# A pipelined image tower on one core: the same pieces in another order on five queues

## The chip, the cores and the metric

The kernel runs on one core of a Trainium2 chip. The metric is the device time of one execution in microseconds. Three runs of the kernel before took 1986.72, 1967.69 and 1971.06 us, so the median is 1971.06 us.

## The reference

The input x holds 128 images of 64 x 64 positions with 128 channels, in float32. The reference computes, one stage after the other:

```
h = avgpool8x8(depthwise_conv3x3(x, conv_w) + conv_b)           # 64 tokens of 128 channels per image
h = h + attention(layernorm(h))                                  # one head, L0
h = h + shared_experts(n) + top2_of_8_experts(n),  n = layernorm(h)   # hidden width 512, exact gelu
h = h + attention(layernorm(h))                                  # 8 heads, rotary, 64 own + 15 pooled keys + sink, L1
h = h + W2 @ gelu(W1 @ layernorm(h) + b1) + b2                   # channel mixing, L1
```

The output is 128 x 64 x 128 values in float32. x is 268 MB, and it is read once.

## The kernel before, in words

**Groups and stages.** The images are taken in 16 groups of eight (512 tokens, four tiles of 128). A group passes through four stages: tok (load, pool, convolution), att (first attention and the gate of the experts), ffn (experts) and sec (second attention and channel mixing). The loop over i is a software pipeline. In iteration i, tok works on group i, att on i-1, ffn on i-2 and sec on i-3 (function `stages`). There are 19 iterations, 0 to 18, and all four stages are at work in iterations 3 to 15. Work named with a mark (out') belongs to the iteration before and is done in the next.

**The order.** Each engine runs one written list of pieces in each iteration, the dict ORDER at lines 57 to 97: `sp` for SyncE, `pe` for TensorE, `act` for ScalarE, `dve` for VectorE, `pool` for GpSimd. A piece is a few instructions with the semaphore waits that they need. Within an engine nothing overtakes, and between engines only semaphores bind. So the order decides what a wait holds up, and the data flow does not depend on it.

**The pieces of tok.** load.u.v (line 378) brings 2 MB of x into one of two buffers (v), four times in a group (u); before it SyncE waits until TensorE has read what the buffer held. pair (DVE, L1063), two add (GpSimd, L1363), inner (ACT L759, then DVE L1067) and pool (PE, L446, L449, L454) follow on each load. tap.p.n (DVE, L1084, L1091) are the 30 steps of the convolution on pooled data, out (PE L418) turns the result.

**The pieces of att.** att.0 (DVE moments, then GpSimd, L1335), att.1 (DVE L1055, then PE and ACT) and on to att.12; high, low and rest split the normalised rows in two bf16 halves; scatter.0 to 7 (GpSimd, L1352) write the rows to their experts' places in memory.

**The pieces of ffn.** up.q and down.q are the shared experts. moe (DVE L1215) takes their sum out of the bank that lift.0 then writes. For each of 15 blocks of 128 rows there are lift.j (PE L564, ACT L836), widen.j (PE L579 to L581, ACT L845 with gelu), narrow.j (PE L591, L595, ACT L855) and store.j (SyncE, L404, 64 KB). Both expert weights of a block are found by a register that TensorE reads at the head of widen (`value_load`, L571). rows.0 to 2 (L397) bring back the scattered rows. Two banks alternate: widen.j waits until narrow.j-2 has been copied out. There are five output slots: narrow.j on ScalarE waits until store.j-5 has landed (L854).

**The pieces of sec.** gather.0 to 7 (GpSimd, L1374) wait for all 15 stores, mix adds, pre.1 to pre.7 and split make keys and values, score.n, exp, turn.n and value.n are the attention in eight halves, post.0 to post.5 the rest. score.0 waits for split and for pre.7 on ScalarE; value.n+1 waits for value.n on VectorE; exp waits for score.7.

**SyncE's queue.** One list holds loads and stores. A store that is issued behind a load lies behind its 2 MB.

## Time and profile before

| | us |
|---|---|
| median of three runs | 1971.06 |
| the profiled execution | 2000.31 |
| its span, first to last instruction | 1998.4 |
| iterations 0 to 2 (filling the pipeline) | 0 to 295 |
| iterations 3 to 15 (all stages) | 295 to 1698 |
| iterations 16 to 18 (draining) | 1698 to 1998 |

The iterations are told apart by the first matmul of up.0 (L526). The profiled execution is 29 us longer than the median of the runs. TensorE is busy 85% of the span, VectorE 65%, ScalarE 54%, GpSimd 38%. The mean granted TensorE clock is 0.932 of full speed. An engine's idle time is listed in front of the instruction that ended it, with what released it.

### The profile page before, as it was taken

To read this page: it belongs to the slowest core of one execution; us is meant where nothing else is said; L and a number is where in the kernel's file an instruction comes from. 1 tells how busy PE (TensorE), PEld (TensorE's weight loads), DVE (VectorE), ACT (ScalarE), POOL (GpSimd) and SP (SyncE) were. 2 spreads that over 40 slices of the span, in tenths; PEclk is the share of its full clock that TensorE was granted. 3 is DMA by queue.
4 is the path that set the end of the run, shared out by engine and by line. 5 is a ranking of instruction groups with operands and counts; after the bars stand their busy time and mean duration, and the time that the engine had idled before them with its cause. 6 is when DMAs were issued, how large, how long until landed. Compare 5 with 4: busy or idle time off the path is not lost.

```text
span 1998.4 us, 42920 instructions
## 1 busy us (share of the span) xinstructions
...
## 2 busy tenths in 40 slices
...
PEclk9999989999899999799998999999999999988775
...
GB/s 253 223 172 261 164 209 194 184 176 183 219 182 176 202 203 173 153 174 191 181 187 206 183 196 205 176 186 206 163 208 185 203 164 147 43 15 53 12 22 6
DMA packets 109125, 331.56 MB, mean 166 GB/s; under 512 B 13662, under 2 KB 87585, under 8 KB 92412
## 3 DMA queue, kind: packets, MB, share of 16 engines
...
## 4 chain that ended last, share of the span: by engine, by line
PE 42%; POOL 19%; DVE 14%; issue 13%; ACT 6%; DMA 4%; ACTq 1%; another core or an unknown queue 0%; SPq 0%; POOLq 0%; DVEq 0%
PE hid_bank L595 7%; POOL yg L1374 7%; PE sec_bank L649 5%; POOL rows_d L1352 5%; PE pool_bank L449 3%; POOL xbuf L1363 3%; PE sec_bank L669 3%; PE sec_bank L660 3%; PE hid_bank L580 3%; PE hid_bank L579 3%; PE pool_bank L454 2%; DVE xc L1268 2%; POOL rs L1335 2%; DVE x L1055 2%; PE hid_bank L581 2%
## 5 line engine op out<-in xcount | busy, mean ns | idle before, releaser
L1363 POOL TENSOR_TENSOR xbuf<-xbuf 128x512 f32<-128x512 f32 x256 | 328.2, 1282 | 633.0 <-DVE xbuf L1063 621.7
L845 ACT ACTIVATE hid<-hid_bank,bias_t 128x128 f32<-128x128 f32 x960 | 273.1, 371 | 116.0 <-PE hid_bank L581 113.6
L595 PE MATMUL hid_bank<-w_s,hid 128*128 x1920 | 291.2, 297 | 0.0
L595 PEld LDWEIGHTS hid_bank<-w_s,hid 128*128 128x128 f32 x1920 | 244.4, 199 | 16.9
L1084 DVE SCALAR_TENSOR_TENSOR taps<-pooled_s,tapw,taps 128x256 f32<-128x256 f32 (+1 forms) x416 | 240.5, 578 | 10.6
L1063 DVE TENSOR_TENSOR xbuf<-xbuf 128x1536 f32<-128x1536 f32 x128 | 224.0, 1750 | 30.4 <-DMA xbuf<-in_x 30.3
L579 PE MATMUL hid_bank<-xt,w_b 128*128 128x128 bf16 x960 | 213.2, 234 | 35.0 <-issue 17.1
L580 PE MATMUL hid_bank<-xt,w_b 128*128 128x128 bf16 x960 | 213.5, 234 | 0.7
L581 PE MATMUL hid_bank<-xt,w_b 128*128 128x128 bf16 x960 | 209.5, 230 | 0.0
L1374 POOL DMA_INDIRECT yg<-outs_d,spot_i x128 | 151.2, 1182 | 54.7 <-issue 38.8
L1067 DVE TENSOR_TENSOR xbuf<-xbuf 128x512 bf16<-128x512 f32 x128 | 102.1, 797 | 98.4 <-ACT xbuf L759 94.6
L1352 POOL DMA_INDIRECT rows_d<-x2r,spot_i x128 | 130.8, 1022 | 88.3 <-DVE owned L1210 51.3
L759 ACT ACTIVATE xbuf<-xbuf 128x512 bf16<-128x512 f32 x128 | 80.8, 631 | 138.4 <-POOL xbuf L1363 137.6
L449 PE MATMUL pool_bank<-block_sum,xbuf 128*128 128x48 f32 x1024 | 151.8, 295 | 0.0
L579 PEld LDWEIGHTS hid_bank<-xt,w_b 128*128 x960 | 97.7, 102 | 78.7 <-issue 71.4
L855 ACT ACTIVATE ys<-hid_bank 128x128 f32<-128x128 f32 x240 | 67.1, 280 | 148.8 <-PE hid_bank L595 130.0
L454 PE MATMUL pool_bank<-block_sum,xbuf 128*128 128x48 f32 x1024 | 144.9, 293 | 0.0
L828 ACT ACTIVATE hid<-hid_bank,b_s 128x512 f32<-128x512 f32 x128 | 85.6, 686 | 107.1 <-PE hid_bank L528 80.1
L1335 POOL TENSOR_TENSOR rs<-ve,power 128x4 f32<-128x4 f32 x64 | 77.7, 1214 | 171.1 <-DVE ve L1048 170.6
L1055 DVE TENSOR_SCALAR x<-h,mv,rs 128x128 f32<-128x128 f32 x192 | 86.3, 511 | 81.3 <-POOL rs L1335 81.3
L449 PEld LDWEIGHTS pool_bank<-block_sum,xbuf 128*128 128x128 f32 x1024 | 138.4, 210 | 0.0
L454 PEld LDWEIGHTS pool_bank<-block_sum,xbuf 128*128 128x128 f32 x1024 | 137.9, 212 | 0.4
...
## 6 DMA issues: line engine op xcount, KB each, us to landing
xbuf<-in_x SPq DMA_DIRECT2D x128, 2048.0 KB
...
rows_d<-x2r,spot_i POOLq DMA_INDIRECT x128
yg<-outs_d,spot_i POOLq DMA_INDIRECT x128
```

Of the source, the lines that this page charges most:

```text
L449: mm = nc.tensor.matmul(view[:, 1, :, side[bx]], blocks[v][:, bx, 0, :], block_sum[:], start=True, stop=True)
L454: mm = nc.tensor.matmul(view[:, :, v, side[bx]], blocks[v][:, bx, 7, :], block_sum[:], start=True, stop=True)
L579: nc.tensor.matmul(out_q, w_high, high, start=True, stop=False)
L580: nc.tensor.matmul(out_q, w_low, high, start=False, stop=False)
L581: mm = nc.tensor.matmul(out_q, w_high, low, start=False, stop=True)
L595: mm = nc.tensor.matmul(hid_bank[n % 2][:, 0:P], hid[:, n % RING, q * P:(q + 1) * P], w_q, start=False, stop=q == FC - 1)
L845: ins = nc.scalar.activation(hid[:, n % RING, cols], hid_bank[n % 2][:, cols], ACT.Gelu, bias=bias_t[:, q, j:j + 1])
L1063: nc.vector.tensor_tensor(v[:, :, 1:6:2, :], v[:, :, 1:6:2, :], v[:, :, 2:7:2, :], ALU.add) \
L1084: nc.vector.scalar_tensor_tensor(dst, src, w, dst, ALU.mult, ALU.add).then_inc(tapped, 1)
L1352: nc.gpsimd.indirect_dma_start(out=rows_d, out_offset=bass.IndirectOffsetOnAxis(spot_i[b][:, k:k + 1], 0), in_=x2r[b][:, k % T, :], in_off ...
L1363: nc.gpsimd.tensor_tensor(v[:, :, 1, :], v[:, :, 1, :], v[:, :, 2 * k + 3, :], ALU.add) \
L1374: nc.gpsimd.indirect_dma_start(out=yg[:, n, :], out_offset=None, in_=outs_d, in_offset=bass.IndirectOffsetOnAxis(spot_i[b][:, n:n + 1], 0)) \
```

## The change

Only the lists in ORDER change. All pieces stay, with the instructions in them and the waits. Three kinds of pieces also change the iteration in which they are done: store.4 and store.6 (SyncE; now at the end of their own iteration), scatter.6 (GpSimd) and tap.1.7, tap.1.8 (VectorE), now at the head of the next.

```
 sp (after):
+        store.8' store.9' store.11' store.7' store.10' load.0.0 store.12' store.13' store.14' load.0.1 rows.0
+        rows.1 load.1.0 load.1.1 rows.2 store.2 store.0 load.2.0 load.2.1 store.1 load.3.0 store.3 load.3.1
+        store.6 store.4 store.5 keep.0
 pe (after):
+        up.0 table up.1 up.2 up.3 down.0 down.1 up.4 up.5 down.2 down.3 down.4 out' up.6 up.7 down.5 down.6
+        down.7 pool.0.0 lift.0 pool.0.1 lift.1 widen.0 pool.0.2 widen.1 lift.2 narrow.0 lift.3 att.1 narrow.1
+        pool.0.3 widen.2 lift.4 pre.2 att.2 pre.3 widen.3 lift.5 att.3 narrow.2 lift.6 pre.4 narrow.3 pool.1.0
+        pre.5 pool.1.1 pre.6 pre.7 widen.4 att.4 pool.1.2 widen.5 lift.7 score.0 score.1 lift.8 pool.1.3 narrow.4
+        score.2 score.3 att.7 lift.9 score.4 score.5 narrow.5 score.6 score.7 att.8 widen.6 pool.2.0 pool.2.1
+        widen.7 turn.0 narrow.6 turn.1 pool.2.2 value.0 widen.8 turn.2 value.1 narrow.7 turn.3 pool.2.3 att.10
+        value.2 lift.10 turn.4 value.3 widen.9 turn.5 att.11 lift.11 value.4 narrow.8 turn.6 lift.12 value.5
+        widen.10 lift.13 narrow.9 turn.7 value.6 narrow.10 att.12 value.7 widen.11 widen.12 post.0 lift.14
+        narrow.11 post.1 widen.13 pool.3.0 pool.3.1 narrow.12 pool.3.2 pool.3.3 widen.14 narrow.13 post.3
+        narrow.14 post.4 post.5
 act (after):
+        hidden.0 hidden.1 table hidden.2 hidden.3 hidden.4 hidden.5 inner.0.0 out' hidden.6 hidden.7 pool.0.0
+        lift.0 inner.0.1 lift.1 widen.0 lift.2 widen.1 narrow.0 att.1 lift.3 pool.0.2 pre.2 widen.2 narrow.1
+        att.2 lift.4 lift.5 pool.0.3 widen.3 lift.6 narrow.2 inner.1.0 pre.5 att.3 pre.6 split narrow.3 pre.7
+        inner.1.1 pool.1.0 lift.7 widen.4 att.6 pool.1.2 lift.8 widen.5 att.7 narrow.4 inner.2.0 pool.1.3
+        narrow.5 gate exp widen.6 pool.2.0 turn.0 lift.9 inner.2.1 narrow.6 widen.7 turn.1 turn.2 narrow.7 turn.3
...
 dve (after):
+        pair.0.0 tap.1.7' tap.1.8' tap.1.9' tap.1.10' tap.1.11' tap.1.12' tap.1.13' tap.1.14' inner.0.0 pair.0.1
+        att.0 moe att.1 mix inner.0.1 pre.1 pre.2 pair.1.0 pre.3 pre.5 inner.1.0 pre.4 pair.1.1 att.4 att.5
+        inner.1.1 score.0 score.1 pair.2.0 score.2 score.3 score.4 att.7 score.5 inner.2.0 score.6 score.7
+        pair.2.1 att.8 tap.0.0 att.9 tap.0.1 value.0 tap.0.2 tap.0.3 inner.2.1 att.10 tap.0.4 tap.0.5 value.1
+        value.2 tap.0.6 pair.3.0 value.3 gate tap.0.7 value.4 att.11 value.5 pair.3.1 rest value.6 inner.3.0
+        value.7 att.12 tap.0.8 tap.0.9 tap.0.10 inner.3.1 post.1 low tap.0.11 post.2 post.3 tap.0.12 tap.0.13
...
 pool (after):
+        scatter.6' scatter.7' gather.0 gather.1 gather.2 add.0.0 gather.3 add.0.1 gather.4 gather.5 gather.6
+        gather.7 add.0.2 att.0 add.0.3 pre.1 add.1.0 add.1.1 pre.3 pre.4 add.1.2 add.1.3 add.2.0 add.2.1 add.2.2
+        add.2.3 att.9 add.3.0 add.3.1 add.3.2 add.3.3 scatter.0 scatter.1 scatter.2 post.1 post.2 scatter.3
+        scatter.4 scatter.5 weights.0 ...
```

The lists before, for the places that the prediction compares:

```
 sp:   store.6' store.7' store.4' store.9' store.10' store.8' load.0.0 store.13' store.11' store.12' store.14'
       load.0.1 rows.1 rows.0 load.1.0 load.1.1 store.1 rows.2 load.2.0 store.0 store.2 load.2.1 store.3
       load.3.0 load.3.1 store.5 keep.0
 pe:   ... pool.0.0 pool.0.1 down.6 down.7 pool.0.2 lift.0 att.1 lift.1 widen.0 lift.2 widen.1 att.2 narrow.0 lift.3
       pool.0.3 lift.4 widen.2 ... pre.4 att.4 pre.5 pre.6 lift.7 pre.7 widen.3 pool.1.0 pool.1.1 widen.4 pool.1.2
       score.0 score.1 ... score.7 lift.8 att.8 widen.6 narrow.5 turn.0 widen.7 turn.1 pool.2.0 lift.9 value.0
       pool.2.1 narrow.6 ... att.11 widen.10 turn.7 lift.12 narrow.9 value.6 narrow.10 value.7 ...
       widen.13 widen.14 pool.3.3 narrow.13 post.3 narrow.14 post.4 post.5
 act:  ... pre.5 inner.1.0 pre.6 pre.7 split att.6 widen.3 ... exp lift.8 narrow.5 inner.2.0 turn.0 widen.6 ...
 dve:  ... att.0 att.1 moe mix pre.1 inner.0.1 pre.2 pair.1.0 pre.5 pre.3 pre.4 ... value.5 att.11 value.6 inner.3.0
       rest value.7 pair.3.1 att.12 ...
 pool: ... gather.7 att.0 add.0.2 add.0.3 pre.1 ...
```

## Rows read from the trace of the kernel before

**Rows 1.** The page: span, and TensorE's granted clock in 40 slices (tenths).

```profile
span 1998.4 us, 42920 instructions
...
PEclk9999989999899999799998999999999999988775
```

**Rows 2.** Busy time by stretch: length, PE, PEld, DVE, ACT, POOL busy, clock, DMA.

```profile
295.20:1698.10 1402.90, 1314.99 (x12103) 1031.94 (x12104) 1052.12 (x2593) 857.27 (x2184) 612.78 (x506) 0.95 0.52 186
...
1084.60:1088.00 3.40, 3.40 (x12) 1.76 (x11) 2.62 (x5) 1.18 (x5) 0.75 (x1) 0.50 0.02 5
```

**Rows 3.** TensorE's waits in iterations 3 to 15: total us, times, longest.

```profile
PE down_bank L564 <- DVE h L1215: 23.5, 13, 3.3
```

**Rows 4.** ScalarE's waits for a landed store, same stretch.

```profile
ACT ys L855 <- DMA outs_d<-ys: 5.8, 7, 1.2
```

**Rows 5.** VectorE in time in iteration 10: start, length, what, idle before.

```profile
1076.50 3.15 DVE L1055 TENSOR_SCALAR x<-h,mv,rs 128x128 f32<-128x128 f32 x4 [2.74 <-POOL rs L1335]
1079.57 0.68 DVE L1215 TENSOR_TENSOR h<-down_bank,h 128x512 f32<-128x512 f32 x1
...
1085.38 1.11 DVE L1055 TENSOR_SCALAR x<-h,mv,rs 128x128 f32<-128x128 f32 x4 [0.91 <-POOL rs L1335]
```

**Rows 6.** GpSimd in time in the same stretch: two additions.

```profile
1076.45 2.60 POOL L1363 TENSOR_TENSOR xbuf<-xbuf 128x512 f32<-128x512 f32 x2
```

**Rows 7.** TensorE in time: lift.0 and the first matmul of widen.1.

```profile
1080.31 0.29 PE L564 MATMUL down_bank<-ident_b,rows_s 128*128 128x128 bf16 x2 [0.93 <-DVE h L1215]
...
1083.79 0.23 PE L579 MATMUL hid_bank<-xt,w_b 128*128 128x128 bf16 x1 [0.49 <-issue]
```

**Rows 8.** TensorE: starts of widen.3, pool.1.0, pool.1.1, widen.4, pool.1.2.

```profile
1102.12 0.23 PE L579 MATMUL hid_bank<-xt,w_b 128*128 128x128 bf16 x1 [0.20 <-issue]
...
1103.14 0.36 PE L446 MATMUL pool_bank<-block_b,xbuf 128*128 128x48 bf16 x8
...
1104.25 1.06 PE L454 MATMUL pool_bank<-block_sum,xbuf 128*128 128x48 f32 x8
1105.14 0.22 PE L579 MATMUL hid_bank<-xt,w_b 128*128 128x128 bf16 x1
...
1105.82 0.60 PE L454 MATMUL pool_bank<-block_sum,xbuf 128*128 128x48 f32 x4
```

**Rows 9.** ScalarE: pre.7, split, exp, a table load and widen.6.

```profile
1102.89 1.53 ACT L899 ACTIVATE values<-sec_bank 15x256 f32<-15x256 f32 x4
1104.44 2.57 ACT L884 ACTIVATE keys_h<-roped,heads 128x512 f32<-128x512 f32 x4
...
1119.09 2.49 ACT L907 ACTIVATE e<-e 128x1280 f32<-128x1280 f32 x2
...
1123.61 1.28 ACT L845 ACT_TABLE_LOAD   x1
1124.91 1.14 ACT L845 ACTIVATE hid<-hid_bank,bias_t 128x128 f32<-128x128 f32 x4
```

**Rows 10.** TensorE: narrow.9, value.6 and value.7 by their starts.

```profile
1143.68 0.23 PE L591 MATMUL hid_bank<-bias_b,owned 24*128 24x128 bf16 x1
...
1144.92 0.65 PE L669 MATMUL sec_bank<-values,p3t 80*64 80x17 f32 x16
...
1146.74 0.65 PE L669 MATMUL sec_bank<-values,p3t 80*64 80x17 f32 x16
```

**Rows 11.** VectorE: taps beside additions, value.6, rest, pair.3.1.

```profile
1126.98 1.82 DVE L1084 SCALAR_TENSOR_TENSOR taps<-pooled_s,tapw,taps 128x224 f32<-128x224 f32 x2
...
1146.11 0.23 DVE L1285 TENSOR_TENSOR x<-sec_bank,inv 128x64 f32<-128x64 f32 x1
...
1146.85 0.69 DVE L1131 TENSOR_TENSOR x2r<-k,x2r 128x512 bf16<-128x512 f32 x1
...
1147.81 1.75 DVE L1063 TENSOR_TENSOR xbuf<-xbuf 128x1536 f32<-128x1536 f32 x1
```

**Rows 12.** The last iteration: VectorE's pre.5.

```profile
1932.23 3.20 DVE L1268 SCALAR_TENSOR_TENSOR xc<-x3t,cg,xc 128x120 f32<-128x120 f32 x7
```

More of the change, by code:

```diff
@@ L62 @@
     pe="""
-        up.0 up.1 table up.2 up.3 down.0 down.1 down.2 up.4 down.3 up.5 out' up.6 down.4 down.5 up.7 pool.0.0
-        pool.0.1 down.6 down.7 pool.0.2 lift.0 att.1 lift.1 widen.0 lift.2 widen.1 att.2 narrow.0 lift.3 pool.0.3
-        lift.4 widen.2 pre.2 narrow.1 pre.3 lift.5 att.3 lift.6 narrow.2 pre.4 att.4 pre.5 pre.6 lift.7 pre.7
-        widen.3 pool.1.0 pool.1.1 widen.4 pool.1.2 score.0 score.1 att.7 score.2 score.3 narrow.3 score.4
-        pool.1.3 score.5 widen.5 narrow.4 score.6 score.7 lift.8 att.8 widen.6 narrow.5 turn.0 widen.7 turn.1
@@ L68 @@
-        pool.2.0 lift.9 value.0 pool.2.1 narrow.6 turn.2 lift.10 pool.2.2 att.10 widen.8 value.1 turn.3 value.2
-        narrow.7 turn.4 pool.2.3 value.3 lift.11 widen.9 turn.5 value.4 narrow.8 turn.6 value.5 att.11 widen.10
-        turn.7 lift.12 narrow.9 value.6 narrow.10 value.7 widen.11 att.12 lift.13 post.0 widen.12 pool.3.0 post.1
-        narrow.11 pool.3.1 pool.3.2 narrow.12 lift.14 widen.13 widen.14 pool.3.3 narrow.13 post.3 narrow.14
-        post.4 post.5""",
-    act="""
-        hidden.0 hidden.1 table hidden.2 hidden.3 inner.0.0 hidden.4 out' hidden.5 hidden.6 hidden.7 pool.0.0
-        inner.0.1 lift.0 pool.0.2 lift.1 att.1 widen.0 lift.2 widen.1 lift.3 narrow.0 att.2 pool.0.3 lift.4 pre.2
-        widen.2 lift.5 narrow.1 att.3 lift.6 gate narrow.2 pre.5 inner.1.0 pre.6 pre.7 split att.6 widen.3
-        inner.1.1 pool.1.0 pool.1.2 widen.4 narrow.3 att.7 pool.1.3 lift.7 widen.5 narrow.4 exp lift.8 narrow.5
-        inner.2.0 turn.0 widen.6 lift.9 turn.1 narrow.6 turn.2 widen.7 high att.10 lift.10 inner.2.1 turn.3
-        pool.2.0 pool.2.2 narrow.7 widen.8 turn.4 turn.5 widen.9 pool.2.3 narrow.8 turn.6 lift.11 widen.10 turn.7
-        narrow.9 inner.3.0 lift.12 narrow.10 widen.11 post.0 widen.12 narrow.11 pool.3.0 lift.13 pool.3.2
-        inner.3.1 narrow.12 lift.14 widen.13 widen.14 pool.3.3 narrow.13 post.3 narrow.14 post.4 post.5 weights.0
-        weights.1 weights.2 weights.3 weights.4 weights.5 weights.6 weights.7 weights.8 weights.9""",
@@ L83 @@
-    dve="""
-        tap.1.9' pair.0.0 tap.1.10' tap.1.11' tap.1.12' tap.1.13' tap.1.14' inner.0.0 pair.0.1 att.0 att.1 moe
-        mix pre.1 inner.0.1 pre.2 pair.1.0 pre.5 pre.3 pre.4 att.4 inner.1.0 att.5 pair.1.1 score.0 score.1
-        score.2 inner.1.1 score.3 att.7 gate score.4 score.5 pair.2.0 score.6 score.7 att.8 att.9 inner.2.0
-        tap.0.0 att.10 pair.2.1 tap.0.1 tap.0.2 value.0 tap.0.3 tap.0.4 tap.0.5 value.1 inner.2.1 value.2 tap.0.6
-        tap.0.7 tap.0.8 low tap.0.9 value.3 tap.0.10 tap.0.11 tap.0.12 value.4 pair.3.0 value.5 att.11 value.6
-        inner.3.0 rest value.7 pair.3.1 att.12 post.1 post.2 inner.3.1 post.3 tap.0.13 tap.0.14 tap.1.0 tap.1.1
-        tap.1.2 tap.1.3 tap.1.4 tap.1.5 tap.1.6 tap.1.7 post.5 tap.1.8 weights.0 weights.1 weights.2 weights.3
-        weights.4 weights.5 weights.6 weights.7 weights.8 weights.9""",
```

19 lines of the change are left out of this document (10 added, 9 removed).

## The prediction

> **What bounds the kernel now.** I read the page first, then the busy time by stretch, then TensorE's waits, then the five engines in time in iteration 10, and the lists beside them. In iterations 3 to 15 TensorE is busy for 1315.0 of 1402.9 us, VectorE for 1052 and GpSimd for 613 [rows 2]. An iteration takes 107.9 us (1402.9 / 13), with 101.2 of it TensorE's. So TensorE is the bound, and another order can gain there only 87.9 us of idle time in all, 6.8 an iteration, and what of its busy time is no matmul at full rate. Two things are of that second kind. The granted clock is 0.95 in this stretch [rows 2]: a few us in each iteration run at 1.2 GHz. One such piece, 3.4 us long, begins at 1084.60 [rows 2], right after TensorE had stood still for 0.93 and 0.49 us ahead of lift.0 and widen.1 [rows 7]. And a widen at whose head TensorE has little queued takes longer, since its register work shows: widen.3 with its gap takes 0.20 + (1103.14 - 1102.12) = 1.22 us, widen.4 only 1105.82 - 1105.14 = 0.68 [rows 8]. The filling and draining (595 us of the span) are chains; the clock falls to 0.5 at the end [rows 1].
>
> The profiled execution took 2000.31 us, 29 more than the median of the runs. The sum is made against 2000.31 and carried over to 1971.06 as a difference.
>
> **Stores and loads (SyncE).** The wait for a landed store at narrow.9 on ScalarE is 5.8 us in 13 iterations [rows 4], behind store.4, which stood at the end of the list behind load.3.1. Now store.4 goes out right behind load.3.1 in its own iteration, and narrow.9 comes later after pool.2.3. TensorE feels at most all of it, 0.45 us an iteration, at least nothing, since ScalarE has room. I take -0.2 (the lists give no reason for a loss). Loads keep their releasers: load.1.0 goes out about 2 us later (pool.0.1 is now behind lift.0), load.1.1, load.2.0, load.2.1 and load.3.0 earlier. Nothing waits for load.1.0 ahead of pair.1.0, which comes after pre.2 in both lists, so I cost this at nothing. If that cover fails, VectorE stands before pair.1.0 and pre.3 is late.
>
> **lift.0 (TensorE, VectorE).** TensorE waits 23.5 us in 13 iterations for moe [rows 3], 1.8 each. moe stands behind att.1, which waits for GpSimd and then takes 3.15 us, against 1.11 for the same four instructions in pre.2 [rows 5]; att.1 runs beside two additions of GpSimd [rows 6]. Now moe is ahead of att.1. After down.7 TensorE has pool.0.0, 1104.25 - 1103.14 = 1.11 us [rows 8], and moe needs 0.68 [rows 5]. The wait goes: -1.8. What is late next is pre.2. On GpSimd att.0 is now behind add.0.2 (half of 2.60 [rows 6]), and att.1 meets one addition instead of two. I find x3 ready within 0.4 us of where TensorE wants it; this is in the small items below.
>
> **Where widen stands (TensorE).** Ahead of widen.1, 2, 3, 7 and 14 there is now a pool piece, or pre.3, on which TensorE works while the registers are read. Each gains 1.22 - 0.68 = 0.54, and widen.1 its gap of 0.49 [rows 7, 8]. widen.4 and 8 lose this cover, widen.10 half of it. Net -(5 x 0.54 + 0.49) + 2.5 x 0.54 = -1.8. Between ends: nothing, and -3.2 if no cover is lost.
>
> **split, narrow.3, pre.7 (ScalarE).** score.0 needs split and pre.7. Before, split was last; now narrow.3 and pre.7 (1.53) follow split (2.57) [rows 9], and att.3 is put in between while inner.1.0 leaves. widen.5 needs narrow.3 and stands ahead of score.0. TensorE's work from pre.5 on is as long as before, but pool.1.1 (0.89 [rows 8]) moved ahead of pre.6, so ScalarE starts pre.6 later. The bounds are 0 and 1.53 + 0.28 = 1.8 (0.28 is my estimate of narrow.3's copy). I take +1.1, nearest to pool.1.1's 0.89 and the extra piece.
>
> **exp, widen.6, narrow.6 (ScalarE).** Before, narrow.5, turn.0 and much more stood between exp and narrow.6. Now TensorE has only turn.0 between exp's end and narrow.6, and ScalarE has the gelu table load 1.28 and widen.6 1.14 there [rows 9]. If TensorE arrived with exp, it would wait 2.42 less turn.0's 0.4, 2.0 us. It has widen.6, two pool pieces and widen.7 ahead of turn.0 as cover, some 1.2 us more than before, but ScalarE has gate and its table load ahead of exp. Between 0.2 and 2.0, I take +1.0.
>
> **att.11, pair.3.1, rest, value.6 (VectorE).** Before, value.6 followed att.11 and ended at 1146.34, 0.40 us ahead of value.7 on TensorE (1146.74) [rows 10, 11]. Now pair.3.1 (1.75) and rest (0.69) are in front of it [rows 11]: 2.44 more. TensorE has narrow.8 more between att.11 and value.7, 1144.92 - 1143.68 = 1.24 [rows 10]. So it waits 2.44 - 1.24 - 0.40 = 0.8; bounds 0 and 2.44. The handing over between engines adds 0.1, so I take +0.9.
>
> **Small items.** up.3 (table moved), pre.2, narrow.5, turn.2, value.3: each within 0.2 us; together +0.5.
>
> **Ends of the run.** scatter.6 leaves iteration 1 ahead of the expert weights, about 1 us on the chain: -1. In the draining iterations pre.3 is now ahead of pre.5 on VectorE. pre.5 (3.2 us and a first instruction [rows 12]) used to run while TensorE did pre.3, and pre.7 (1.53 [rows 9]) used to be ahead of split. In iteration 18, with nothing to cover it, I find score.0 1.5 us later; iteration 17 adds the same kind of wait and a longer one at narrow.6, iteration 16 little. Together +4; bounds 0 and 3 x 3.5.
>
> **The sum.** -0.2 - 1.8 - 1.8 + 1.1 + 1.0 + 0.9 + 0.5 = -0.3 an iteration, times 13 is -4. The clock: the piece at 1.2 GHz behind lift.0 costs half of 3.4, 1.7 us, in most iterations; the three new waits are of about the same length as the 0.93 that preceded it and may each draw one. I take a gain of 0.5 an iteration, -6. With -1 and +4 the sum is -7: 2000.3 becomes 1993, and the median 1971.06 becomes **1964 us**.
>
> **The rivals.**
> - *Faster.* The new waits stay at their lower bounds (0, 0.2, 0) because ScalarE and VectorE, both with idle time left in [rows 2], run ahead. Then an iteration gains 0.2 + 1.8 + 1.8 - 0.2 - 0.5 = 3.1, and 0.5 by the clock: 13 x 3.6 = 47, less 3 at the ends: 1927. For it: the gains are seen in rows, the losses are worked out from lists. Against: two of the losses have no room at all between producer and reader.
> - *Slower.* The clock. It fell behind 0.93 and 0.49 us of idle time [rows 7]. If it falls in the same way behind two of the three new waits (narrow.6, score.0, value.7), each costs 1.7 us, and the piece behind lift.0 stays for widen.0's sake. An iteration then loses 3.4 - 0.3 = 3.1, 13 x 3.1 + 3 = 43: 2014. It decides from one new piece at 1.2 GHz an iteration on. Against: each new wait is a single one, while those ahead of the fall were two gaps with an exposed widen.0 between them.
> - *The additions block rest.* Taps that follow a pair beside GpSimd's additions take 0.91 each (1.82 for two [rows 11]), and att.1 shows the same [rows 5]. rest now follows pair.3.1 at once and falls into add.3.2 and add.3.3, while before it ran clear. If it waits out one whole addition, half of 2.60 [rows 6], value.7 waits 1.3 us more: 13 x 1.3 = 17, so 1981. The Trainium skill, SBUF — State Buffer, section Who interferes with whom, states that rule: a VectorE instruction with two SBUF inputs contends with a GpSimd instruction that reads SBUF, and whoever comes second is blocked until the other is done. The trace agrees on the taps; by that rule the wait at value.7 is 2.2 us in place of 0.9.
> - *The change doesn't do what it says.* As many stores stand behind a load as before, and what they cost is 5.8 us [rows 4]. If nothing else moved either, the time is 1971.
>
> **How the numbers follow.** Forecast 0.33, faster 0.30, slower 0.22, blocked rest 0.10, no effect 0.05. A measurement of this kernel can tell about 1%, 20 us, from no change. Faster by more: 0.31. Within: 0.47. Slower: 0.22. The range reaches past the faster rival's time and nearly to the slower's, 1920 to 2010; about 1 in 10 is left out on each side.
>
> **What would show it.** Right: no wait of L564 for L1215; the first of widen.1, 2, 3, 7 and 14 without a gap; new waits of TensorE at L591 for ACT L845 and at L669 for DVE L1285, each near 1 us; score.0 waiting for L899, not L884. Wrong: new pieces at 1.2 GHz 40, 60 or 85 us into an iteration (then slower), or none of the new waits (then faster), or a wait of ScalarE for a store.

## The result: slower, with more of the time at the low clock

| | before | after |
|---|---|---|
| median of 4 runs, us | 1978.9 | 2031.8 |
| lowest to highest | 1967.7 to 1990.1 | 2010.7 to 2045.9 |
| profiled execution, us | 2000.3 | 2025.0 |

The ratio of after to before is 1.0227, with a 95% interval of 1.0158 to 1.0295. This ratio, like those below, leaves out runs more than 1.5% above the fastest of their kernel (here 2045.9 us), so it is not the ratio of the two medians. The forecast was 1964 us in a range of 1920 to 2010, with a chance of 0.22 for slower: the result lies outside the range, on the side of the rival called *Slower*.

The page of the kernel after, first: its span, its busy time, and TensorE's granted clock in 40 slices. It answers to [rows 1].

```profile
span 2023.1 us, 42920 instructions
...
PE 1750.1 (87%) x14896; PEld 1359.8 (67%) x14896; DVE 1253.4 (62%) x3244; ACT 1068.5 (53%) x2707; POOL 782.0 (39%) x643
...
PEclk9999999988979797888979799989999899999575
```

The middle of the row, which was nearly all nines, now has sevens and eights. The same in numbers, by stretch, for iterations 3 to 15 (290.6 to 1731.5 us; it answers to the first line of [rows 2]): us, busy time and count of each engine, granted clock, DMA share, GB/s.

```profile
290.60:1731.50 1440.90, 1368.79 (x12104) 1067.38 (x12105) 999.79 (x2586) 856.76 (x2184) 639.42 (x509) 0.91 0.51 181
```

The stretch is 1440.9 - 1402.9 = 38.0 us longer, with the same matmuls in it. TensorE's idle time fell from 87.9 to 72.1 us, and its busy time rose by 53.8. The granted clock fell from 0.95 to 0.91. Counted in the records of the clock, TensorE had 127.2 us at 1.2 GHz in this stretch before and 262.8 after. The two stretches shown below hold 129 matmuls in 27.3 us at 1.2 GHz and 270 in 25.0 us at 2.4, so work at 1.2 GHz takes about twice its time, and half of the difference, 67.8 us, is lost to the clock. What is left, 38.0 - 67.8 = **-29.8 us, is my estimate of what the new order gained, 2.3 us an iteration**. It is rough. Iterations 11 and 15 of after, with no time at 1.2 GHz, take 101.2 and 101.1 us, against 104.3 for the only such iteration of before (14), which says 3.1. And the same sum applied to runs that keep the order of before (e4, e16 and e17 below) is off by 0.6 to 0.9 us an iteration. Outside this stretch the kernel after is 13.3 us shorter (4.6 ahead of it, 8.7 behind it).

TensorE's waits in that stretch, longest sums first: us in total, times, longest. They answer to [rows 3] and [rows 7].

```profile
PE hid_bank L579 <- issue: 22.8, 52, 0.7
PE hid_bank L579 <- ACT ys L855: 14.4, 25, 0.9
PE hid_bank L579 <- ACT xt L836: 13.9, 20, 2.1
PE sec_bank L691 <- ACT o3t L922: 10.1, 13, 0.8
PE hid_bank L526 <- ACT hid L828: 4.8, 12, 0.4
PE pool_bank L418 <- DVE cols L1091: 2.4, 5, 0.5
PE sec_bank L645 <- ACT values L899: 1.1, 7, 0.2
...
PE down_bank L564 <- DVE h L1215: 0.2, 1, 0.2
```

The wait at lift.0 is down from 23.5 us to 0.2. A new one stands at a widen (L579) for a copy of narrow (L855): 13 of its 25 instances, 11.0 us of the 14.4, are widen.5 waiting for narrow.3, 0.8 to 0.9 us in each of 13 iterations. The waits at L579 for nothing shown (issue) and for a copy of lift (L836) were 11.0 and 6.7 us before; the widens are taken up again below. Now two iterations of the kernel after, in order of time on TensorE (start, length, instruction, and in brackets the idle time before it and what ended it). First widen.5 and score.0 of iteration 10, then those of iteration 11.

```profile
1133.09 0.23 PE L579 MATMUL hid_bank<-xt,w_b 128*128 128x128 bf16 x1 [0.89 <-ACT ys L855]
1134.53 0.30 PE L645 MATMUL sec_bank<-limit_b,place_b 67*128 67x320 bf16 x1
...
1246.44 0.23 PE L579 MATMUL hid_bank<-xt,w_b 128*128 128x128 bf16 x1 [0.83 <-ACT ys L855]
1247.89 0.30 PE L645 MATMUL sec_bank<-limit_b,place_b 67*128 67x320 bf16 x1 [0.16 <-ACT values L899]
```

The two look alike. What follows does not. The same kernel by stretch, the score phase and the turns of iteration 10 and of iteration 11:

```profile
1137.80:1165.10 27.30, 27.30 (x129) 18.52 (x128) 12.90 (x32) 16.06 (x38) 6.22 (x5) 0.50 0.37 137
1250.00:1275.00 25.00, 24.67 (x270) 19.05 (x266) 18.75 (x52) 21.64 (x52) 6.23 (x5) 1.00 0.52 185
```

For 27.3 us TensorE is busy without a gap and gets 129 matmuls done at a granted 0.50, against 270 in 25 us at 1.00. Iteration 10 takes 117.7 us and iteration 11 takes 101.2. Eight iterations of the 13 (4 to 10 and 12) have such a piece of 23.9 or 27.3 us; it begins 1.5 to 4.7 us behind the wait. Before, only one iteration of 3 to 15 had one (27.3 us, in iteration 7, 69 us into it, in the turns). The best iterations of before take 103.6 us, those of after 101.1.

### The profile page after: what moved, and what is told of

It is laid out like the page before. It is cut to its first block, busy times and chain, and to the rows that moved or that the text cites. A ratio compares the mean times of both kernels' runs of the same rounds, so it can differ in the third digit from the quotient of the medians.

```text
span 2023.1 us, 42920 instructions
## 1 busy us (share of the span) xinstructions
PE 1750.1 (87%) x14896; PEld 1359.8 (67%) x14896; DVE 1253.4 (62%) x3244; ACT 1068.5 (53%) x2707; POOL 782.0 (39%) x643
## 4 chain that ended last, share of the span: by engine, by line
PE 67%; ACT 10%; issue 8%; POOL 7%; DMA 3%; DVE 3%; ACTq 2%; POOLq 0%
PE hid_bank L595 14%; PE sec_bank L649 5%; PE pool_bank L449 5%; PE pool_bank L454 4%; PE hid_bank L580 4%; POOL yg L1374 4%; PE hid_bank L579 4%; PE down_bank L540 3%; PE sec_bank L660 3%; PE sec_bank L669 3%; PE sec_bank L614 3%; PE hid_bank L581 2%; ACT keys_h L884 2%; PE hid_bank L591 2%; POOL xbuf L1363 2%
## 5 line engine op out<-in xcount | busy, mean ns | idle before, releaser
L1363 POOL TENSOR_TENSOR xbuf<-xbuf 128x512 f32<-128x512 f32 x256 | 338.5, 1322 | 699.1 <-DVE xbuf L1063 690.5
L595 PE MATMUL hid_bank<-w_s,hid 128*128 x1920 | 315.9, 314 | 0.0
L595 PEld LDWEIGHTS hid_bank<-w_s,hid 128*128 128x128 f32 x1920 | 266.4, 215 | 18.2
L579 PE MATMUL hid_bank<-xt,w_b 128*128 128x128 bf16 x960 | 216.9, 235 | 64.5 <-issue 26.9
L580 PE MATMUL hid_bank<-xt,w_b 128*128 128x128 bf16 x960 | 218.0, 236 | 0.5
L581 PE MATMUL hid_bank<-xt,w_b 128*128 128x128 bf16 x960 | 213.2, 230 | 0.0
L1352 POOL DMA_INDIRECT rows_d<-x2r,spot_i x128 | 134.0, 1047 | 103.6 <-DVE owned L1210 70.8
L579 PEld LDWEIGHTS hid_bank<-xt,w_b 128*128 x960 | 99.6, 104 | 98.5 <-issue 87.8
L1067 DVE TENSOR_TENSOR xbuf<-xbuf 128x512 bf16<-128x512 f32 x128 | 93.0, 726 | 117.1 <-ACT xbuf L759 117.1
L449 PEld LDWEIGHTS pool_bank<-block_sum,xbuf 128*128 128x128 f32 x1024 | 145.4, 219 | 0.0
L454 PEld LDWEIGHTS pool_bank<-block_sum,xbuf 128*128 128x128 f32 x1024 | 139.4, 212 | 0.0
L649 PE MATMUL sec_bank<-keys_h,q 64*64 64x316 f32 x512 | 138.1, 628 | 0.0
L772 ACT ACTIVATE pooled_s<-pool_bank 128x384 f32<-128x384 f32 x192 | 94.3, 491 | 80.4 <-PE pool_bank L449 65.7
L836 ACT ACTIVATE xt<-down_bank 128x256 bf16<-128x256 bf16 x240 | 92.2, 384 | 84.3 <-PE down_bank L564 84.1
L1274 DVE TENSOR_REDUCE m<-sec_bank 128x4 f32<-128x320 f32 x128 | 62.5, 488 | 118.8 <-PE sec_bank L649 118.8
```

Of the source, the lines that this page charges most:

```text
L449: mm = nc.tensor.matmul(view[:, 1, :, side[bx]], blocks[v][:, bx, 0, :], block_sum[:], start=True, stop=True)
L454: mm = nc.tensor.matmul(view[:, :, v, side[bx]], blocks[v][:, bx, 7, :], block_sum[:], start=True, stop=True)
L579: nc.tensor.matmul(out_q, w_high, high, start=True, stop=False)
L580: nc.tensor.matmul(out_q, w_low, high, start=False, stop=False)
L581: mm = nc.tensor.matmul(out_q, w_high, low, start=False, stop=True)
L595: mm = nc.tensor.matmul(hid_bank[n % 2][:, 0:P], hid[:, n % RING, q * P:(q + 1) * P], w_q, start=False, stop=q == FC - 1)
```

## The experiments

**Theory A**: a short wait of TensorE right ahead of the score phase, or in it, is what the clock falls behind; the fall then lasts for the phase. **Theory B**: the new row of pieces does it, whatever the waits. Theory C, formed on the way: both take a part. Each kernel is named by its edit. "Long pieces" are iterations of 3 to 15 with 13 us or more on end at 1.2 GHz, in the profiled execution. That is one execution of each kernel: for e5 and e9 it is among the longest of their runs, for e6 it is the shortest, so these counts are not averages. "Added wait" is TensorE's wait in or ahead of the score phase. In some of these kernels a list takes a line or two less, and their line numbers are one or two lower.

| kernel | added wait, us | long pieces | iteration, us | at 1.2 GHz, us | ratio to before (95%) |
|---|---|---|---|---|---|
| before | 0.2 | 1 | 107.9 | 127 | 1 |
| after | 0.8 to 0.9 at widen.5 | 8 | 110.8 | 263 | 1.0227 (1.016 to 1.030) |
| e1 | 1.1 to 1.2 at score.0 | 13 | 114.9 | 368 | 1.0493 (1.043 to 1.056) |
| e2 | 1.6 to 1.8 at score.0 | 13 | 117.6 | 369 | 1.0687 (1.062 to 1.076) |
| e3 | 0.2 | 1 | 106.9 | 90 | 0.9944 (0.991 to 0.998) |
| e4 | 0.2 | 1 | 107.2 | 92 | 0.9985 (0.994 to 1.003) |
| e5 | 0.2 | 6 | 110.4 | 244 | 0.9978 (0.993 to 1.002) |
| e6 | 0.2 | 0 | 105.0 | 75 | 0.9896 (0.983 to 0.996) |
| e7 | 3.4 at att.7 | 13 | 116.0 | 352 | 1.0622 (1.056 to 1.068) |
| e8 | 4.0 to 4.2 at score.0 | 13 | 120.9 | 413 | 1.0930 (1.087 to 1.099) |
| e9 | 0.2 | 2 | 106.9 | 137 | 0.9822 (0.977 to 0.987) |
| e10 | 0.2 | 0 | 106.4 | 120 | 1.0015 (0.998 to 1.005) |
| e11 | 1.6 to 1.8 at score.0 | 13 | 119.0 | 382 | 1.0787 (1.074 to 1.084) |
| e12 | 0.2 at score.0 and 0.3 at score.2 (2.5 at score.4 in iteration 9 alone) | 13 | 115.4 | 370 | 1.0603 (1.056 to 1.065) |
| e13 | 0.2 | 1 | 107.9 | 111 | 1.0062 (1.002 to 1.011) |
| e14 | 0.7 to 0.9 at score.0 | 13 | 118.1 | 393 | 1.0669 (1.060 to 1.074) |
| e15 | 0.2 | 0 | 105.8 | 89 | 0.9882 (0.984 to 0.992) |
| e16 | 0.2 | 1 | 107.8 | 101 | 0.9958 (0.992 to 1.000) |
| e17 | 0.2 | 1 | 107.6 | 100 | 0.9989 (0.995 to 1.003) |
| e18 | 0.8 to 0.9 at widen.5 | 6 | 111.0 | 224 | none, see below |

### Does the wait do it? e14, e2, e1

**e14: the kernel before, one piece of TensorE moved.** ScalarE's list is that of before. The move makes the wait, but it also puts widen.4 between score.0 and score.1, so the row of the score phase is not quite that of before.

```
-pe: widen.3 pool.1.0 pool.1.1 widen.4 pool.1.2 score.0 score.1 att.7
+pe: widen.3 pool.1.0 pool.1.1 pool.1.2 score.0 widen.4 score.1 att.7
```

> The kernel before, with widen.4 (0.83 us) behind score.0 on TensorE: TensorE comes to score.0 0.7 to 0.8 us earlier and waits there 0.9 to 1.0 us in place of 0.2; the work up to score.1 and the time of its end are unchanged, so the move costs nothing by itself. Theory A with size (0.9 us made 8 of 13): long pieces in 5 to 13 iterations, ratio 1.02 to 1.05. If it was the new row of pieces and not the wait that made 8 of 13 in the kernel after: as before, ratio 0.997 to 1.005.

Measured: 1.0669. The waits of TensorE (300 to 1690 us), then two lines in order of time in iteration 9, then the same iteration by stretch, up to the fall and in it:

```profile
PE sec_bank L645 <- ACT keys_h L884: 10.0, 12, 0.9
...
1048.53 0.31 PE L645 MATMUL sec_bank<-limit_b,place_b 67*128 67x320 bf16 x1 [0.81 <-ACT keys_h L884]
1048.77 1.32 PE L649 MATMUL sec_bank<-keys_h,q 64*64 64x316 f32 x4
...
1001.20:1048.60 47.40, 41.19 (x313) 31.63 (x310) 32.31 (x67) 25.51 (x59) 25.57 (x21) 0.93 0.50 175
1048.80:1076.10 27.30, 27.30 (x130) 16.22 (x130) 13.05 (x36) 12.98 (x32) 3.03 (x3) 0.50 0.39 153
```

The same stretches of the kernel before, iteration 9:

```profile
951.20:997.70 46.50, 41.82 (x323) 31.41 (x321) 32.08 (x67) 25.42 (x59) 24.05 (x21) 0.96 0.51 178
997.90:1025.20 27.30, 27.01 (x270) 19.94 (x271) 22.48 (x56) 22.90 (x58) 7.08 (x6) 1.00 0.60 231
```

Up to score.0 the two are alike. The four matmuls of L649 behind the wait take 1.32 us in e14 against 0.76 at full clock, and the next 27.3 us hold 130 matmuls against 270. An iteration is 118.1 - 107.9 = 10.2 us longer, and half of the added time at 1.2 GHz, (392.7 - 127.2) / 2 / 13, is 10.2: all of the loss is the clock, and a move that makes 0.7 us more of waiting brought it. e16 below moves another small piece (lift.7) to the same place and makes no wait, and its score phase does not fall (its one long piece begins 68 us into iteration 13, in the turns). Since widen.4 itself stands in the phase now, the wait alone is shown by e2, e8 and e11, which leave TensorE's list as it was: with them theory B is out as the only cause.

**e2: the kernel before, att.6 ahead of split on ScalarE.**

```
-act: pre.6 pre.7 split att.6 widen.3
+act: pre.6 pre.7 att.6 split widen.3
```

> The kernel before, with one move on ScalarE: att.6 stands ahead of split, so that the score phase's input is late in the order of before. TensorE waits some 1.5 us more ahead of score.0 in each of 13 iterations, 20 us in all by itself. Theory A (a short wait at that place brings the clock down for the score and turn phase): long pieces at 1.2 GHz turn up there in most iterations, 2040 us or more, ratio 1.03 or more. Theory B (the row of pieces does it): only the waits themselves, 1985 to 2000 us, ratio 1.00 to 1.01, half-clock time near the 127 us of before.

Measured: 1.0687, as theory A had it. There is a control inside it: TensorE also waits up to 3.3 us at lift.0 there, as it does before [rows 3]. Behind that longer wait stand pieces of 3.4 or 6.8 us at 1.2 GHz; behind the 1.7 us at score.0 stand 17 to 27. So the length of the wait does not decide it alone. The work behind the two waits differs, and so may other things; that it is the work is my reading.

**e1: the kernel after, without its wait at widen.5.**

```
-act: inner.1.0 pre.5 att.3 pre.6 split narrow.3 pre.7
+act: inner.1.0 att.3 narrow.3 pre.5 pre.6 split pre.7
```

> The kernel after, with one move on ScalarE: att.3 and narrow.3 stand ahead of pre.5, so that the copies that widen.5 needs no longer stand behind split (2.57 us). It takes away TensorE's wait of 0.8 to 0.9 us at widen.5 (14.4 us in all). Theory A (this short wait, right ahead of the score phase, is what the granted clock falls behind): the pieces of 23.9 and 27.3 us at 1.2 GHz go from most of the eight iterations that have them; half-clock time in iterations 3 to 15 drops from 262.8 us towards the 127 of the kernel before, which gives back some 68 us, and the waits some 10: 1940 to 1960 us, ratio to before 0.975 to 0.99. Theory B (the new row of TensorE's pieces in that phase is what brings the clock down, whatever the wait): the wait goes but the long pieces stay: 2010 to 2025 us, ratio 1.01 to 1.025.

Measured: 1.0493, worse than either theory said. Its waits of TensorE (iterations 3 to 15), and its fall in iteration 9:

```profile
PE sec_bank L645 <- ACT values L899: 15.4, 13, 1.2
...
1036.00:1056.50 20.50, 20.50 (x92) 12.20 (x92) 12.05 (x25) 13.61 (x30) 4.22 (x4) 0.50 0.28 107
```

I had expected the wait to go. It moved to score.0: ScalarE's chain of pre.5, pre.6, split and pre.7 sets when the scores can begin, and narrow.3 only stood in it. The wait grew from 0.9 to 1.2 us, it now stands directly ahead of the scores, and 13 of 13 iterations fall in place of 8.

### Taking the wait away from the kernel after: e5, e6, e18

**e5** starts TensorE's part of that chain earlier; **e6** takes away the wait at widen.1 too; **e18** does the latter alone.

```
 e5 = e1 and
-pe: narrow.3 pool.1.0 pre.5 pool.1.1 pre.6 pre.7 widen.4
+pe: narrow.3 pre.5 pre.6 pool.1.0 pre.7 pool.1.1 widen.4
 e6 = e5 and, e18 = after and
-act: inner.0.1 lift.1 widen.0
+act: lift.1 inner.0.1 widen.0
```

> The kernel of the experiment with narrow.3 early, and beside it one more move, on TensorE: pre.5, pre.6 and pre.7 stand ahead of pool.1.0 and pool.1.1 by one to two pieces, so that ScalarE's chain of pre.5, pre.6, split and pre.7 starts some 1.3 us earlier and TensorE finds both inputs of the score phase ready. The same pieces, the same lengths at full speed; only the last short wait (1.2 us at score.0 in 13 of 13 iterations) is taken away. Theory A (the granted clock falls behind a wait right ahead of the score phase): the pieces of 20.5 to 27.3 us go, iterations of 100 to 103 us, 1920 to 1950 us, ratio to before 0.965 to 0.985. Theory B (the new row of pieces brings it down whatever the waits): the long pieces stay in half of the iterations or more, 2010 us or more. Theory C (each takes its part): between, 1960 to 2000 us.

> The same as e5, and on ScalarE lift.1 ahead of inner.0.1, which takes away most of TensorE's wait at widen.1 and widen.0 (up to 1.1 us at +20.8, behind which pieces of 3.4 and 6.8 us at 1.2 GHz stand in seven iterations of the kernel after). Theory A: these short pieces go too: 0.6 to 1.5 us less in each of 13 iterations than e5, 8 to 20 us in all. If pieces of 3.4 us come without a wait: within 5 us of e5.

> The kernel after, with lift.1 ahead of inner.0.1 on ScalarE alone: it takes away most of TensorE's waits at widen.0 and widen.1 and leaves the 0.8 to 0.9 us at widen.5. If the wait at widen.5 makes the loss: still 1.01 to 1.03 of before. If the waits at the front of the iteration set it up (e6 was 0.008 under e5 by this move): under 1.005.

Measured: e5 0.9978, e6 0.9896. e18 has no ratio: its four runs took 2014.8 to 2052.8 us, beside 1982.2 to 2014.4 in the 19 of before, so it is slower, and by how much stays open. From e1 to e5 only 1.0 us of waiting at score.0 goes, and 5% with it; long pieces fall from 13 to 6. That is theory A. But six long pieces behind a wait of 0.2 us are more than before ever shows, so a part stays that the wait doesn't explain: theory C. (The profiled execution of e5, 2036.7 us, is one of its longest; but over its shorter ones, 1971.5 to 2000.3 us, the granted clock was 0.916 to 0.935 too, against 0.927 to 0.945 for before beside it. With all 13 runs counted, e5's median is 2000.3 us beside 2001.0 of before, which tells the same.) Two iterations of e5 make it plain that it is not a matter of the iteration's own course: in iterations 7 and 8 score.0 starts 41.3 and 41.2 us into the iteration, with the same wait; the first has no time at 1.2 GHz and takes 102.6 us, the second has 27.3 on end and takes 116.0. With e6's move too, the median is 24 us lower (1976.0), but the two intervals overlap, and of e6's six runs two took 2005 and 2006 us at a clock of 0.917 and 0.918; whether the fall is rarer there is not shown. e18 shows that this move alone doesn't take the loss away while the wait at widen.5 stands.

### The row of pieces: e7, e12

Both meant to put the score phase of e6 back into the order of before, to try theory C.

```
 e6:   score.0 score.1 lift.8 pool.1.3 narrow.4 score.2 score.3 att.7 lift.9 score.4 score.5 narrow.5
 e7:   score.0 score.1 att.7 score.2 score.3 lift.8 narrow.4 score.4 pool.1.3 score.5 lift.9 narrow.5
 e12:  score.0 score.1 score.2 score.3 lift.8 narrow.4 score.4 att.7 pool.1.3 score.5 lift.9 narrow.5
```

> The kernel of e6, with the score phase's row on TensorE put back to that of before as far as its pieces allow: att.7 ahead of score.2, then narrow.4 behind score.3, pool.1.3 ahead of score.5, lift.8 and lift.9 later. Waits of TensorE as in e6 (0.2 us at score.0). Theory C (besides the waits, the row of pieces of the score phase in after's order takes the clock down in a part of the runs): the runs draw together at the lower end, 1955 to 1970 us, granted clock 0.935 or more in all of them. Theory A (waits alone): no difference to e6, 1962 to 2006 us, clocks between 0.917 and 0.941.

> The kernel of e6, with score.2 and score.3 ahead of lift.8 and narrow.4, and pool.1.3 behind score.4: the order of before within the score phase, this time with att.7 late enough that it need not wait 3.4 us for att.6 as in e7. If the row of pieces in that phase is what leaves e6 nearer to a fall than before (clock 0.917 to 0.941 against 0.926 to 0.945): 1955 to 1970 us with clocks over 0.935. If it is not: as e6, 1962 to 2006 us. If a wait over 1 us appears inside the row: over 2050 us with 13 of 13 iterations falling, as e7.

Measured: 1.0622 and 1.0603. e7 made a wait of its own inside the phase, 3.4 us at att.7 for att.6 in all 13 iterations, and is one more case of theory A.

e12 is another matter. Its waits of TensorE in iterations 3 to 15 at the scores (L643 there), the starts of score.0 to score.3 in iteration 10, and the fall behind them:

```profile
PE sec_bank L643 <- DVE e L1274: 6.9, 15, 2.5
PE sec_bank L643 <- ACT values L897: 2.7, 13, 0.2
...
1161.36 0.30 PE L643 MATMUL sec_bank<-limit_b,place_b 67*128 67x320 bf16 x1 [0.21 <-ACT values L897]
1162.28 0.31 PE L643 MATMUL sec_bank<-limit_b,place_b 67*128 67x320 bf16 x1
1163.58 0.31 PE L643 MATMUL sec_bank<-limit_b,place_b 67*128 67x320 bf16 x1 [0.30 <-DVE e L1274]
1164.50 0.31 PE L643 MATMUL sec_bank<-limit_b,place_b 67*128 67x320 bf16 x1
...
1164.90:1192.20 27.30, 27.30 (x138) 19.69 (x137) 13.09 (x32) 15.42 (x36) 6.23 (x5) 0.50 0.35 128
```

TensorE waits 0.2 us at score.0, as in e6, and 0.3 at score.2, for the bank that VectorE's work on the scores frees. In 12 of 13 iterations the long piece begins 0.6 to 1.4 us behind that. The 2.5 us at score.4 stand in iteration 9 alone, the one that had not fallen before. So e6's kernel with another row in the score phase, and with 0.3 us of waiting more, falls in 13 of 13 where the trace of e6 has none. Row and wait can't be told apart here, but a wait of 0.7 us isn't needed. This speaks for theory C.

### How small a wait does it? e8, e11, e13, e16, e17

```
 before's act:  gate narrow.2 pre.5 inner.1.0 pre.6 pre.7 split att.6 widen.3 inner.1.1
 e8:            gate narrow.2 pre.5 inner.1.0 pre.6 pre.7 inner.1.1 split att.6 widen.3
 e11:           pre.5 inner.1.0 pre.6 pre.7 narrow.2 gate split att.6 widen.3 inner.1.1
 e13:           gate pre.5 inner.1.0 pre.6 pre.7 narrow.2 split att.6 widen.3 inner.1.1
 e16: act as before; pe: lift.7 from behind pre.6 to behind score.0
 e17: e13's act, e16's pe
```

> The kernel before, with inner.1.1 (0.65 us) ahead of split on ScalarE: a third of the delay that att.6 (1.63 us) made. TensorE should wait 0.7 to 0.8 us at score.0 in place of 0.2. Theory A: long pieces at 1.2 GHz in a part of the iterations, as behind the 0.9 us of the kernel after (8 of 13): 2020 to 2080 us, ratio 1.015 to 1.045. Theory B (the row does it): 1990 to 2005 us, ratio 1.00 to 1.005. If the fall has a threshold between 0.8 and 1.2 us: as theory B.

> The kernel before, with narrow.2 and gate (0.26 and 0.23 us) behind pre.7 and ahead of split on ScalarE. In e8 the piece moved ahead of split stood waiting itself and made 4.1 us out of an intended 0.7; here both pieces are ready long before, so TensorE should wait 0.6 to 0.8 us at score.0 in place of 0.2. Theory A with a size to it (0.9 us: 8 of 13 iterations fall; 1.2 us and over: 13 of 13): long pieces in 3 to 10 iterations, 2000 to 2060 us, ratio 1.01 to 1.035. If waits under a microsecond do nothing: 1980 to 1995 us, ratio 1.00 to 1.005.

> The kernel before, with narrow.2 alone (0.26 us) behind pre.7 and ahead of split on ScalarE, without gate, in front of which ScalarE spent 1.3 us that e11's expectation had left out. TensorE should wait 0.4 to 0.5 us at score.0. If the fall grows with the wait: 1 to 6 of 13 iterations with a long piece, ratio 1.003 to 1.02. If there is a step between 0.5 and 0.9 us: as before, 0.997 to 1.005. If any wait over the usual 0.2 us is enough: 13 of 13, ratio over 1.04.

> The kernel before, with lift.7 (0.27 us on TensorE) behind score.0: TensorE comes to score.0 some 0.25 us earlier and should wait 0.3 to 0.45 us there in place of 0.2. If the fall has a step above that: ratio 0.997 to 1.008, at most 2 long pieces in 13 iterations. If it grows evenly with the wait: 3 to 6 of 13, ratio 1.01 to 1.025.

> e16, and narrow.2 (0.26 us) behind pre.7 on ScalarE as in e13: a wait of 0.5 to 0.65 us at score.0. If the step lies below: 10 to 13 of 13 and a ratio over 1.04, as with 0.9 us in e14. If above: as before. If even: 5 to 8 of 13, 1.02 to 1.035.

All five missed the size that they aimed at. In e8 inner.1.1 stood at the head of ScalarE's queue and waited itself: 4.1 us. In e11 ScalarE spent 1.3 us ahead of gate on its table: 1.8 us. Both fell in 13 of 13; in e8 the low clock begins even before the wait ends, by 0.1 to 3.0 us. In e13, e16 and e17 there was no added wait at all, perhaps because what was moved was small beside what the two engines had to spare (not shown), and there the time stayed within 1% of before. So there are points at 0.2 us (0 or 1 iteration in the order of before) and at 0.7 to 0.9 (13 of 13), and none between: whether there is a step is open. On another row, that of e12, 0.2 and 0.3 us were enough.

### The prediction's own terms: e3, e4, e9, e10, e15

**e3: moe ahead of att.1, nothing else. e4: SyncE's new list, nothing else.**

```
 e3
-dve: att.0 att.1 moe mix
+dve: att.0 moe att.1 mix
 e4: before, with the sp list of after
```

> The kernel before, with moe ahead of att.1 on VectorE and nothing else. TensorE's wait at lift.0 (23.5 us over 13 iterations, 1.8 each) goes or shrinks to a few tenths. If the prediction's term holds: minus 20 us directly and half-clock time down by the short pieces that stand behind that wait, 1940 to 1955 us, ratio 0.98 to 0.99. If the wait moves to the next piece that att.1 feeds: 1970 to 1980 us, ratio 1.00. Theory A leaves room for a loss only if a new short wait stands ahead of the score phase, and none is made here.

> The kernel before, with SyncE's order of the kernel after and nothing else: the stores' triggers stand two to three places away from the loads of x. The prediction's term: minus 0.2 us in each of 13 iterations, ScalarE's waits for outs buffers (5.8 us in 7) gone, TensorE hardly touched: 1975 to 1982 us beside a median of 1979, ratio 0.995 to 1.003. If the stores' place bounds TensorE anywhere: under 1960 us. If the loads get late behind stores: over 1990 us, with PE waits for x at the head of an iteration.

Measured: 0.9944 and 0.9985. The stores are worth nothing that can be measured. e3 gains 1.0 us an iteration where the term said 1.8 and the clock 0.5 more, and the 37 us less at 1.2 GHz, 1.4 us an iteration by half of them, can account for all of it. Its waits of TensorE (295 to 1690 us) say why nothing else came:

```profile
PE att_bank L417 <- DVE x L1054: 24.9, 13, 2.5
PE hid_bank L525 <- ACT hid L827: 20.6, 21, 2.5
```

The wait for moe has become one of the same size for att.1, the next piece on TensorE behind lift.0.

**e9: the front of the iteration alone.** **e10** adds the head of the iteration of after, **e15** adds the sp list of after.

```
 e9 = e3 and
-pe:  pool.0.2 lift.0 att.1 lift.1 widen.0 lift.2 widen.1 att.2 narrow.0 lift.3 pool.0.3 lift.4
+pe:  pool.0.2 lift.0 lift.1 widen.0 lift.2 widen.1 att.1 narrow.0 lift.3 pool.0.3 att.2 lift.4
-act: inner.0.1 lift.0 pool.0.2 lift.1 att.1 widen.0 lift.2 widen.1 lift.3 narrow.0 att.2 pool.0.3
+act: lift.0 lift.1 inner.0.1 pool.0.2 widen.0 lift.2 widen.1 att.1 lift.3 narrow.0 pool.0.3 att.2
 e10 = e9 and, from the kernel after,
+pe:  up.0 table up.1 up.2 up.3 down.0 down.1 up.4 up.5 down.2 down.3 down.4 out' up.6 up.7 down.5 down.6
+     down.7 pool.0.0 pool.0.1 pool.0.2 lift.0
+act: hidden.3 hidden.4 hidden.5 inner.0.0 out' hidden.6 hidden.7
```

> The kernel before, with only the part of the change ahead of widen.2: moe ahead of att.1 on VectorE, att.1 behind widen.1 on TensorE, lift.0 and lift.1 ahead of inner.0.1 on ScalarE. Waits of TensorE at lift.0 (1.8 us an iteration) go and none takes their place at att.1 (1.9 in the run with moe alone); the score phase stays as it was, with 0.2 us ahead of score.0. The prediction's term: minus 1.8 us in each of 13 iterations and the short pieces at 1.2 GHz behind lift.0, 0.5 each: minus 30 us in all, 1960 to 1975 us beside some 2000 on a chip like the last, ratio 0.98 to 0.99. If the wait only moves on: 0.995 to 1.00.

> The kernel of e9, and beside it the head of the iteration in the order of the kernel after: table, up, down and out' on TensorE (with pool.0.0 to pool.0.2 all behind down.7), hidden and inner.0.0 on ScalarE. In e9 TensorE waits 19.9 us in 24 places at up for hidden and 8.3 us at pool.0 for VectorE's sums between 300 and 1690 us. If these waits shrink as in the kernel after (4.8 us for hidden): minus 10 to 20 us against e9, ratio to before 0.972 to 0.978. If the wait only moves to lift.0 or to down.5, as e3's did: within 5 us of e9, 0.98 to 0.985.

> The kernel of e9 (0.982 of before), with SyncE's order of the kernel after beside it. The stores alone gave 0.9985 with an interval of 0.9936 to 1.0034 on the order of before. If they are free here too: 0.978 to 0.984. If the loads get late behind stores in the shorter iteration: over 0.985.

Measured: e9 **0.9822 (0.9774 to 0.9869), a median of 1949.8 us beside 1981.4 of before: it beats both kernels**. The profiled execution of e9, 1972.6 us, is the longest of its six. e15, the same with the stores moved, gave 0.9882, with an interval that overlaps e9's. e10 gave 1.0015, 2% behind e9: with the head of after its waits for hidden are as large as e9's (19.9 us), and its runs show a granted clock of 0.912 to 0.931 against 0.925 to 0.952 in e9's. Why the clock is lower there stays open. e9's waits of TensorE (300 to 1690 us):

```profile
PE hid_bank L525 <- ACT hid L827: 19.9, 24, 3.1
...
PE pool_bank L445 <- DVE xbuf L1066: 8.3, 8, 1.7
...
PE sec_bank L644 <- ACT keys_h L883: 1.5, 8, 0.2
```

No wait for moe or att.1 is left; those for hidden rose from 14.4 to 19.9 us and one for VectorE's sums came (8.3 us); and score.0 waits 0.2 us at most, as before. In the kernel after, widen.5 waits 0.8 to 0.9 us ahead of it.

## Why the prediction was wrong, step by step

- **The clock: this is the step that failed.** The prediction saw that the new waits "may each draw one" of the pieces at 1.2 GHz, and priced one at 1.7 us, half of the 3.4 us piece behind lift.0 [rows 2, 7]; with the piece behind lift.0 gone it took a gain of 6 us. Measured, a piece behind the wait at widen.5 lasts 23.9 or 27.3 us and costs 12 to 14 us by half of its length (iteration 12, with 23.9 us and no other piece, is 10.4 us longer than iteration 11 with none), and eight iterations have one; by half of the added time at 1.2 GHz the stretch loses 68 us. The price was read from the nearest wait, not from the work that stood behind the wait to be made. The trace of before had samples of the right size, and I did not use them: the piece of 27.3 us in iteration 7, and, nearer to the case, one in iteration 16, outside the stretch that I read. There TensorE waited 1.4 us at score.0, and at once 23.9 us at 0.50 follow:

```profile
1743.34 0.45 PE L645 MATMUL sec_bank<-limit_b,place_b 67*128 67x320 bf16 x1 [1.41 <-ACT keys_h L884]
...
1743.30:1767.20 23.90, 23.86 (x100) 12.64 (x101) 10.36 (x28) 11.52 (x29) 0.00 (x0) 0.50 0.01 3
```

- **The rival *Slower*** had the mechanism and the sign, from the point it named (a new piece at 1.2 GHz), at 1.7 us for each of two pieces: 3.1 us an iteration, against 2.9 measured. The agreement of the two sums is chance: behind it stand one wait in place of two, pieces seven times as long in 8 of 13 iterations, and an order that gained 2.3 us where the rival gave it 0.3.
- **lift.0**: right in the kernel after, where the wait went from 23.5 to 0.2 us and none for moe or att.1 took its place (for widen.1 see below). e3 shows that the reason given was half of it: moe's move only pays because att.1 stands behind narrow.0 and lift.3 on TensorE in the kernel after.
- **Stores**: right. ScalarE's copy of narrow (L855) no longer waits for a landed store; the group's line for iterations 3 to 15, beside [rows 4]:

```profile
L855 ACT ACTIVATE ys<-hid_bank 128x128 f32<-128x128 f32 x195 | 55.0, 282 | 95.2 <-PE hid_bank L595 93.5
```

- **split, narrow.3, pre.7**: +1.1 forecast, 0.8 to 0.9 at widen.5 and up to 0.2 at score.0 measured. The size was right; what it set off was not.
- **Where widen stands (-1.8)**: wrong in sum. widen.2, 3 and 7 lost their gap and are each 0.5 us shorter, as forecast; widen.14 is not. And widen.1 waits 9.7 us in 13 iterations in place of 3.5, now for the copy of lift.1, and widen.12, which the prediction doesn't name and which now follows widen.11 at once, 8.2 in place of 0.1; widen.8, 10 and 11 are longer too. The idle time ahead of all widens but widen.5 is 40.3 us where it was 22.3, 1.4 us an iteration more:

```profile
PE hid_bank L579 <- issue: 11.0, 40, 0.5
...
PE hid_bank L579 <- ACT xt L836: 6.7, 12, 0.7
```

  These two lines are of before; those of after stand in the section on the result (22.8 and 13.9).
- **narrow.6 (+1.0) and value.7 (+0.9)**: wrong. TensorE waits 0.1 us at most at either, in the iterations without a long piece too (3, 11, 13 to 15). The two were to be the larger part of the losses. With them gone the order comes out near the rival *Faster*: 3.1 forecast by it, 2.3 by the estimate above. That is in part luck, since the rival keeps the gain at the widens, which did not come.
- **Blocked rest**: wrong. rest takes 0.68 to 0.69 us in all 13 iterations, as before, though it follows pair.3.1 at once. In iteration 10 it starts at 1182.81 and GpSimd's two additions at 1182.97, behind it, and it is these that are long: 3.32 us for the two, where the two of 1175.44 took 2.77. The prediction asked what blocks rest, not which of the two comes first. att.1 did get shorter, 3.15 to 2.06 us, with one addition of GpSimd beside it in place of two [rows 5, 6]; it is in the mean of this group of VectorE (156 instructions, 524 ns each before):

```profile
L1055 DVE TENSOR_SCALAR x<-h,mv,rs 128x128 f32<-128x128 f32 x156 | 57.9, 434 | 59.1 <-POOL rs L1335 59.1
```

- **Ends**: +3 forecast, -13.3 measured: 4.6 ahead of the stretch and 8.7 behind it, where iteration 16 takes 97.1 us in place of 108.3. That iteration has 13.7 us at 1.2 GHz after and 27.3 before, so 6.8 of its 11.2 us is the clock by half of the difference. The rest of the ends was not looked into.
- **The odds**: 0.31, 0.47 and 0.22 came from cases none of which let a piece cost more than 1.7 us. A range to 2010 took the short piece as given; with one long piece of 27.3 us in half of the iterations it would have reached to 1971 + 6.5 x 13.7 = 2060.

Shown: the loss is time at 1.2 GHz (10.2 of the 10.2 us an iteration in e14; 67.8 us of it in a stretch that is 38.0 us longer in after). A longer wait of TensorE in or ahead of the score phase brings the long pieces in 13 of 13 iterations (e1, e7, e2, e8 and e11, the last three by ScalarE's list alone, and e14 with 0.7 us more), and taking 1.0 us of waiting from e1 gives 5% back (e5). The wait isn't the whole cause: with 0.2 us at score.0 the order of e5, which is nearly that of after, falls in 6 of 13 iterations, and e12's row falls in 13 of 13 with 0.3 us more. Estimated, not shown: the order of after is worth some 30 us at an equal clock.

Open: what of the row makes a fall likely, and what a wait between 0.2 and 0.7 us does on one and the same row. Why 0.9 us at widen.5, one piece ahead of the scores, drew 8 and 6 falls of 13 while 0.9 us at score.0 drew 13; in iteration 16 of after even 1.4 us at widen.5 drew none. And what set off the piece of 27.3 us in iteration 7 of before, ahead of which TensorE waits 0.1 us at most for 20 us.
